# Four exponent buffers, an earlier first attention, and the second normalisation moved ahead of chunk 6's rounding

## What is computed

```
x = x + q8(layernorm(x)) @ q8(context)
x = x + mx_ffn(layernorm(x))            # silu(x Wg) * (x Wu), then Wd; weights fp4, rows fp6, blocks of 32
x = x + attention(layernorm(x), context)  # 32 query heads, 8 key/value heads of 128, rope, softmax
x = x + ffn(layernorm(x))               # 1376 hidden
```

## Time and profile before

| | |
|---|---|
| median of 3 runs | 683.6 us (683.54 to 683.84) |
| profiled execution | 683.66 us |
| its span | 681.9 us |
| PE busy | 659.7 us (97%) |
| DVE busy | 518.0 us (76%) |
| POOL busy | 471.5 us (69%) |
| ACT busy | 344.7 us (51%) |

### The profile page before, as it was taken

How to read it: one execution, slowest core, us unless ns; L and a number is a source line. 1 busy time by engine, 2 the same in 40 slices (tenths; PEclk the granted TensorE clock), 3 DMA queues, 4 the chain that set the end, 5 groups by cost and what they waited for, 6 DMA issues and landing times.

```text
span 681.9 us, 10810 instructions
## 1 busy us (share of the span) xinstructions
PE 659.7 (97%) x2993; PEld 484.8 (71%) x2996; DVE 518.0 (76%) x1024; ACT 344.7 (51%) x665; POOL 471.5 (69%) x435
## 2 busy tenths in 40 slices
PE   9998999899799999999999999999999999899998
PEld 3443444446567888888888888888888877788886
DVE  5999797997788888888888888888888886621113
ACT  1795223424656656656656656556656663221111
POOL 0688937337598688688788788698688477066661
PEclk9999999999999999999999999999999999999999
DMA  8999678403222222222222121222224012012321
GB/s 315 390 343 248 200 195 185 155 1 123 92 79 77 63 78 78 62 79 75 62 79 75 62 84 70 62 77 77 62 78 138 17 32 83 10 48 94 110 73 62
DMA packets 61260, 73.15 MB, mean 107 GB/s; under 512 B 25265, under 2 KB 33585, under 8 KB 60209
## 3 DMA queue, kind: packets, MB, share of 16 engines
q1 hardware_dynamic: 61232, 72.83, 34.7%
HBM read 58.00 MB, written 9.44 MB: 99 GB/s over the span
## 4 chain that ended last, share of the span: by engine, by line
PE 73%; DVE 12%; POOL 7%; issue 4%; ACT 2%; DMA 1%; SPq 0%; POOLq 0%; DVEq 0%; ACTq 0%
PE ps L687 16%; PE ps L689 16%; PE ps L688 16%; PE ps L755 11%; PE ps L721 7%; PE ps L572 3%; PE ps L540 2%; POOL mx_raw L1153 2%; PE ps L608 2%; POOL mx_w L1162 2%; DVE mx_amax L1416 1%; DVE stats L1329 1%; DVE xhat L1358 1%; POOL prob L1230 1%; DMA X<-in_x 1%
## 5 line engine op out<-in xcount | busy, mean ns | idle before, releaser
L1230 POOL TENSOR_SCALAR prob<-prob,rinv 128x512 f32<-128x512 f32 x128 | 89.4, 698 | 72.4 <-DVE rinv L1594 72.3
L1049 ACT ACTIVATE prob<-ps,nmax 128x512 f32<-128x512 f32 x128 | 88.3, 690 | 97.8 <-DVE nmax L1587 95.3
L755 PE MATMUL ps<-xt,wq_sb 128*128 128x512 f32 x384 | 103.1, 393 | 0.1
L1060 ACT CAST pT<-ps 128x512 fp32r<-128x512 f32 x128 | 75.1, 587 | 51.4 <-PE ps L721 50.4
L1587 DVE CUSTOM_DVE_ANT_0 ps<-ps,mask_sb 128x512 f32<-128x512 f32 x128 | 87.8, 686 | 5.1 <-PE ps L689 5.0
L1610 DVE TENSOR_TENSOR pT<-ps,pT 128x512 fp32r<-128x512 f32 x128 | 86.2, 674 | 3.0 <-ACT pT L1060 2.0
L755 PEld LDWEIGHTS ps<-xt,wq_sb 128*128 128x128 f32 x384 | 71.8, 188 | 17.2 <-issue 1.0
L721 PE MATMUL ps<-idf,prob 128*128 128x128 f32 x512 | 76.7, 272 | 0.4 <-POOL prob L1230 0.3
L721 PEld LDWEIGHTS ps<-idf,prob 128*128 128x128 f32 x512 | 63.8, 142 | 17.3 <-POOL prob L1230 1.6
L687 PE MATMUL ps<-pT,vt 128*128 128x512 f32 x128 | 61.2, 478 | 0.9 <-DVE pT L1610 0.9
L540 PE MATMUL ps<-ctxT,wk_sb 128*128 128x512 f32 x128 | 57.7, 594 | 0.0
(11 more groups left out here) (177 smaller groups left out, 1542.3 us busy)
## 6 DMA issues: line engine op xcount, KB each, us to landing
mx_raw<-in_mxw SPq DMA_DIRECT2D x8, 1024.0 KB, 6.9
wq_raw<-in_wq SPq DMA_DIRECT2D x32, 256.0 KB, 3.2
wo_raw<-in_wo SPq DMA_DIRECT2D x32, 256.0 KB, 2.6
v_scr<-v_st SPq DMA_DIRECT2D x16, 256.0 KB, 3.9
k_scr<-k_st SPq DMA_DIRECT2D x16, 256.0 KB, 3.4
kr<-k_scr SPq DMA_DIRECT2D x16, 256.0 KB, 2.8
kr_swp<-k_scr SPq DMA_DIRECT2D x32, 128.0 KB, 3.3
vr<-v_scr SPq DMA_DIRECT2D x16, 256.0 KB, 3.4
```

The lines of the kernel that those rows point to most:

```text
L755: last = mm(query_bank(H), wq_sb[:, par, l, k], xt[:, r, k], start=(n == 0), stop=(n == 11))
L1049: nc.scalar.activation(prob[:, j], bank(j % 2), ACT.Exp, bias=nmax[:, j:j + 1], scale=-1.0, accum_out=rsum[:, j:j + 1]).then_inc(exps, 1)
L1060: copy(pT[:, v % 2, 0, :, i * P:(i + 1) * P], bank(2 + i % 2).rearrange("p (k c) -> p k c", k=4)).then_inc(ph_ready, 1)
L1230: nc.gpsimd.tensor_scalar(prob[:, i], prob[:, i], rinv[:, i:i + 1], 1.0, ALU.mult, ALU.mult).then_inc(probs, 1)
```

## The change

- `mx_e` has four buffers, so that `mx_exponents(i)` waits for `scale_out` of chunk i-4.
- The clip of the first rows goes from DVE to POOL, behind `scale_in(1)`.
- DVE's `attention0` stands at the end of steps 3 and 4, where it was in steps 4 and 5. It adds the product to X first; POOL's `rows_add` adds the share behind it (`l0_read`), and moves from before `scale_out(3)` and `scale_out(4)` to before `scale_in(6)` and `scale_in(7)`. ACT's `share(0)` stands ahead of `context_keep(1)`.
- The second `layernorm`, with its fp6 part, stands ahead of the rounding of chunk 6.
- SP issues `chunk_turn(5)` ahead of the stores of k41, v60 and v61, and the rows' transposes ahead of v61, v70.
- Third stage: the mask operation of score 0 stands earlier on DVE, its exponential ahead of the swap copies of head 2 on ACT, POOL's sine product of head 0 between the two halves of head 2's weight split, and one of three late key products one unit earlier on PE.

```diff
--- before
+++ after
@@ -60,6 +60,7 @@
 NRAW = 3
+NEXP = 4
 ROTATE = (4, 5, 6, 7)
@@ -150,7 +151,7 @@
             mx_amax = sb("mx_amax", [P, CH // BLK], F32, a)
-            mx_e = sb("mx_e", [P, NRAW, CH // BLK], F32, a)
+            mx_e = sb("mx_e", [P, NEXP, CH // BLK], F32, a)
             mx_r = sb("mx_r", [P, NRAW, CH // BLK], F32, a)
@@ -413,12 +414,11 @@
             first_keys_load()
-            stores(STEPS[5][1] + STEPS[6][0])
             chunk_turn(5)
-            stores(STEPS[6][1])
+            stores(STEPS[5][1] + STEPS[6][0][:1])
             rows_turn_again(0)
             rows_turn_again(1)
-            stores(STEPS[7][0])
+            stores(STEPS[6][0][1:] + STEPS[6][1] + STEPS[7][0])
             k_load(6)
@@ -783,8 +783,8 @@
                     query(U, u, j)
-                    if isinstance(U, int) and U == -1 and j == 3:
-                        late_keys(4, range(1, 4))
+                    if isinstance(U, int) and U in (-2, -1) and j == 3:
+                        late_keys(4, range(1, 2) if U == -2 else range(2, 4))
                     if j % 2 == 0:
@@ -970,8 +970,8 @@
             copy_keys(2, 1)
+            share(0)
             context_keep(1)
-            share(0)
             copy_values(4, 0)
@@ -1061,6 +1061,8 @@
                 for j in range(4):
+                    if isinstance(U, int) and U == 0 and j == 0:
+                        exponent(0, 0, 0)
                     if j == 0 and within(U + 2, NH):
@@ -1078,7 +1080,8 @@
                     probs_high(U, u, j)
-                    exponent(U, u, j)
+                    if not (isinstance(U, int) and U == 0 and j == 0):
+                        exponent(U, u, j)
                     if j == 2 and within(U + 2, NH):
@@ -1146,7 +1149,7 @@
                 pool.wait_ge(mx_expo, i + 1)
-                ts(mx_r[:, p, 0:m].bitcast(I32), mx_e[:, p, 0:m].bitcast(I32), -1.0, -(2.0 ** 24), ALU.mult, ALU.add).then_inc(mx_scale, 1)
+                ts(mx_r[:, p, 0:m].bitcast(I32), mx_e[:, i % NEXP, 0:m].bitcast(I32), -1.0, -(2.0 ** 24), ALU.mult, ALU.add).then_inc(mx_scale, 1)
                 pool.wait_ge(mx_scale, i + 1)
@@ -1156,7 +1159,7 @@
                     pool.wait_ge(WT_in[i - 2], 16)
-                p, e = i % 2, i % NRAW
+                p, e = i % 2, i % NEXP
                 for cols in halves(i):
@@ -1181,16 +1184,20 @@
                     pool.wait_ge(l0_shared, t + 1)
+                    pool.wait_ge(l0_read, t + 1)
                     tt(X[:, t], X[:, t], xhat[:, t], ALU.add).then_inc(l0_added, 1)
...
             scale_in(1)
+            pool.wait_ge(q1_rounded, 1)
+            rows = xhat[:].rearrange("p t d -> p (t d)")
+            ts(rows, rows, ROUND, ROUND + 255.0, ALU.max, ALU.min).then_inc(q1_clipped, 1)
             for i in range(NFULL):
+                if i in (L0_AT, L0_AT + 1):
+                    rows_add(i - L0_AT)
                 if i + 2 <= NFULL:
                     scale_in(i + 2)
-                if i in (L0_AT - 1, L0_AT):
-                    rows_add(i - L0_AT + 1)
                 scale_out(i)
@@ -1200,9 +1207,11 @@
-            def split(high, low, raw, h_done, l_done, count):
+            def split(high, low, raw, h_done, l_done, count, between=None):
                 pool.sem_inc(pool_past_wait, 1)
                 nc.gpsimd.tensor_scalar(high, raw, 1.0, 1.0, ALU.mult, ALU.mult).then_inc(h_done, 1)
+                if between:
+                    between()
                 pool.wait_ge(h_done, count)
@@ -1213,12 +1222,17 @@
-            def query_split(U, u, g):
+            def query_sine(U):
+                pool.wait_ge(q_swapped, U + 3)
+                tt(q_swp[:].rearrange("p (b c) -> p b c", b=BATCH), q_swp[:].rearrange("p (b c) -> p b c", b=BATCH),
+                   ropeQ[:, 1].unsqueeze(1).to_broadcast([P, BATCH, SEQ]), ALU.mult).then_inc(q_sined, 1)
+
+            def query_split(U, u, g, between=None):
                 H, par = U + 4, u % 2
...
                     after(pool, q_sums, H - 1)
-                    split(wq_sb[:, par, 0], wq_sb[:, par, 1], wq_raw[:, par], wqh_ready, wq_split, H + 1)
+                    split(wq_sb[:, par, 0], wq_sb[:, par, 1], wq_raw[:, par], wqh_ready, wq_split, H + 1, between)
@@ -1228,12 +1242,12 @@
                         nc.gpsimd.tensor_scalar(prob[:, i], prob[:, i], rinv[:, i:i + 1], 1.0, ALU.mult, ALU.mult).then_inc(probs, 1)
-                    if isinstance(U, int) and U in (-2, -1) and j == 0:
-                        query_split(U, u, g)
-                    if j == 0 and within(U + 2, NH):
-                        pool.wait_ge(q_swapped, U + 3)
-                        tt(q_swp[:].rearrange("p (b c) -> p b c", b=BATCH), q_swp[:].rearrange("p (b c) -> p b c", b=BATCH),
-                           ropeQ[:, 1].unsqueeze(1).to_broadcast([P, BATCH, SEQ]), ALU.mult).then_inc(q_sined, 1)
+                    if isinstance(U, int) and U == -2 and j == 0:
+                        query_split(U, u, g, lambda: query_sine(-2))
+                    elif j == 0 and within(U + 2, NH):
+                        if isinstance(U, int) and U == -1:
+                            query_split(U, u, g)
+                        query_sine(U)
                     if j == 1 and not (isinstance(U, int) and U in (-2, -1)):
@@ -1382,10 +1396,6 @@
-            def clip_rows():
-                dve.wait_ge(q1_rounded, 1)
-                ts(rows(xhat[:]), rows(xhat[:]), ROUND, ROUND + 255.0, ALU.max, ALU.min).then_inc(q1_clipped, 1)
-
             def clip_context(b):
@@ -1402,7 +1412,6 @@
                     dve.wait_ge(l0_sums, 2 * b + t % 2 + b + 2)
-                    dve.wait_ge(l0_added, t + 1)
                     stt(X[:, t], bank(rotating(("l", b, t % 2 + 1))), sx[:, 4:5], X[:, t], ALU.mult, ALU.add).then_inc(l0_read, 1)
@@ -1416,8 +1425,8 @@
             def mx_exponents(i):
-                p, m = i % NRAW, width(i) // BLK
-                after(dve, mx_ready, 2 * (i - NRAW + 1))
+                p, m = i % NEXP, width(i) // BLK
+                after(dve, mx_ready, 2 * (i - NEXP + 1))
                 dve.wait_ge(mx_peak, i + 1)
@@ -1465,15 +1474,10 @@
             for i in range(NFULL):
-                if i != L0_AT + 2:
-                    mx_round(i, 0)
-                    mx_round(i, 1)
+                mx_round(i, 0)
+                mx_round(i, 1)
                 if i + 2 <= NFULL:
                     mx_peaks(i + 2)
-                if i in (L0_AT, L0_AT + 1):
-                    attention0(i - L0_AT)
-                if i == 0:
-                    clip_rows()
                 if i == 2:
@@ -1484,10 +1488,10 @@
                     mx_exponents(i + 2)
+                if i in (L0_AT - 1, L0_AT):
+                    attention0(i - L0_AT + 1)
                 if i == L0_AT + 1:
-                    mx_round(i + 1, 0)
-                    mx_round(i + 1, 1)
-                    dve.wait_ge(l0_read, NT)
+                    dve.wait_ge(l0_added, NT)
                     layernorm(False)
@@ -1568,6 +1572,14 @@
+            def row_max(U, u, j):
+                n = 4 * U + j
+                dve.wait_ge(scores, n + 1)
+                dve.sem_inc(dve_past_wait, 1)
+                nc.vector.tensor_tensor_reduce(out=bank(j % 2), in0=bank(j % 2), in1=mask_sb[:, 2 * (u % 2) + j % 2],
+                                               scale=-1.0, scalar=BIG, op0=ALU.add, op1=ALU.min,
+                                               accum_out=nmax[:, j:j + 1]).then_inc(rowmax, 1)
+
             def unit(U, u, g):
@@ -1579,14 +1591,8 @@
                         tt(oT[:, u % 2, 1], bank(4 + u % 2), oT[:, u % 2, 0].bitcast(F32), ALU.subtract).then_inc(o_split, 1)
-                    if within(U, NUNIT):
-
-                        n = 4 * U + j
-                        dve.wait_ge(scores, n + 1)
-                        dve.sem_inc(dve_past_wait, 1)
-                        nc.vector.tensor_tensor_reduce(out=bank(j % 2), in0=bank(j % 2), in1=mask_sb[:, 2 * (u % 2) + j % 2],
-                                                       scale=-1.0, scalar=BIG, op0=ALU.add, op1=ALU.min,
-                                                       accum_out=nmax[:, j:j + 1]).then_inc(rowmax, 1)
+                    if within(U, NUNIT) and not (isinstance(U, int) and U == 0 and j == 0):
+                        row_max(U, u, j)
@@ -1613,6 +1619,8 @@
                         tt(q_cos[:], q_cos[:], q_swp[:], ALU.add).then_inc(q_roped, 1)
+                    if isinstance(U, int) and U == -1 and j == 2:
+                        row_max(0, 0, 0)
                     if j == 2 and within(U + 2, NH):
```

## The result

The changed kernel takes **694.57 us** (median of 4 runs, 693.62 to 694.84) beside 683.72 for the kernel before on the same chip (4 runs, 683.54 to 684.21): ratio 1.0155, 95% interval 1.0137 to 1.0173. It is slower, as forecast, but by 10.9 us and not by 5; the forecast's range ended at 690.8. The profiled execution has a span of 692.6 and a mean granted clock of 0.992 (before 681.9 and 1.000).

The account below looks back on a forecast made before the run. PE-bound, busy 659.7 of 681.9 us, with gate_up's start as the gate: 683.66 + 5.1 (gate_up at 116.1, not 111.04) - 0.1 (third stage) = 688.7, median 0.06 lower, so 688.6 us; range 684.0 to 690.8.

Parts of the forecast that it names:

- (b): Clip of 1.22 us leaves DVE for a free place on POOL; chunk pipeline moves up by about 1.1 us.
- the clock behind the gap: PE after its 7.6 us gap before v71: slower clock loses 1.7 us, bounded by 0 and 3.4.
- the third stage: Mask, exponential, sine and late-product edits after gate_up: -0.1 us, ends -1.9 and +1.2.
- (a): First attention drains earlier: three PE waits of 4.3 us together go, v71 could start at 98.1, not 102.4.
- T: End of chunk 6's rounding on DVE: forecast 104.1, where it was 86.2.
- at least as much as it saved: Case for POOL's clip: without cover between scale_in(1) and scale_in(2), it costs POOL at least what it saved.
- The normalisation against POOL: DVE's second normalisation starts at 80.2, waits for POOL's instructions of 1.9 us, and ends at 99.3.
- rival 2: DVE loses one turn of 1.9 us less to POOL: T 102.2, gate_up 114.2, 686.7 us; chance 0.13.
- Who waits for T: ACT's lifts and k41's copy, PE's v71 (T + 1.6 = 105.7) and SP's key loads wait for chunk 6's rounding.
- T + 12.0: Start of gate_up on PE counted from the end of chunk 6's rounding: T 104.1 gives 116.1.
- SP: Six key loads wait for T; behind them the rows' transpose lands at T + 11.1 = 115.2.

Follow-up runs that it names:

- e1: The changed kernel with the clip of the first rows back on DVE; 691.30 us, ratio 1.0109 to the kernel before.
- e11: The changed kernel with POOL's max and min on xhat replaced by multiply by 1 and add 0; 689.77 us, ratio 1.0091 to the kernel before.
- e5: The changed kernel with clip and second normalisation both back in their old places; 686.68 us, ratio 1.0046 to the kernel before.
- e2: The changed kernel with chunk 6 rounded ahead of the second normalisation again; 689.12 us, ratio 1.0079 to the kernel before.
- e10: The changed kernel with unit v70's products repeated once and a half more, filling PE's wait before v71; 694.08 us, ratio 1.0150 to the kernel before.
- e4: The kernel before with all the third stage's edits and nothing else of the change; 684.89 us, ratio 1.0015.
- e13: e6 with chunk 8's peaks, chunk 6's clip and chunk 8's exponents right behind the second normalisation on DVE; 681.51 us, ratio 0.9963 to the kernel before.
- e8: The kernel before with only the second normalisation moved ahead of chunk 6's rounding; 691.42 us, ratio 1.0109.
- e3: The changed kernel with unit v70 computed twice, filling part of PE's wait before v71; 694.09 us, ratio 1.0146 to the kernel before.
- e6: The changed kernel with clip, second normalisation and third stage all put back; 685.96 us, ratio 1.0029 to the kernel before.

## Why the prediction was right, and where it failed

The direction was right, and so were the waits that were forecast; the time lies 3.8 us above the stated range. The step that failed is (b), POOL's clip taken as free; two terms were mis-sized besides, the clock behind the gap and the third stage.

- **(a) The attention's waits go: right.** v71 could start at 98.1, I wrote; without the clip on POOL (e1) the values before it end at 87.57 + 10.46 = 98.03. What I did not ask is what is late next if only this is done: DVE's rounding of chunk 7, at the same 109 us. In the change itself T hid it.
- **(b) The clip: this step failed.** "The chunk pipeline moves up by about 1.1 us" had POOL's clip hidden in a free place of unstated length. The place was 4.69 us long, by a row of the kernel before that my sum did not use; the clip took 7.07, and the normalisation began at 84.29, not 80.2. That the rest of the step held is shown by e11, which has no clip of xhat at all: there it began at 79.95, 0.9 before e1, where the clip is on DVE. I had named the case ("at least as much as it saved") and given it no price and no rival; the nearest rows, multiplications on POOL, were of other operations.
- **The normalisation against POOL: right, 1.1 us too dear.** Three small rows waited (1.32, 1.83, 1.83), and it took 18.0 us to the rounding's start where I had 19.1; undisturbed it takes 13.7 (85.73 to 99.44 in e5). Of the 1.1, 0.7 are a slip in my sum: four POOL instructions of 1.9 us from 80.6 end at 88.2, and I wrote 88.9. The row at 90.43 has two inputs of SBUF and took 1.83 us beside POOL, where the same operation took 0.16 at 92.69 with POOL at rest. So the rule of the Trainium skill ("SBUF — State Buffer", "SBUF: two separate sides") that I leaned on, by which such a row too waits for GpSimd's whole instruction, agrees with a row now, and rival 2, one turn fewer, is out.
- **Who waits for T: right.** k41's copy ended at T + 1.63 and v71 started at T + 1.68 (I had 1.6). The gap was 5.3 us and not 7.6, because T came 3.1 us later and PE 5.4 (103.5 for 98.1), mostly by its wait at 58.73 and the slow matmuls behind it: with the late pipeline the rows' transposes for the first attention are late (e2 puts the same wait down to q1T). That delay lay inside the later wait: in the change itself it cost nothing.
- **The clock: right in kind, mis-sized.** v71 lost 3.1 us, not 1.7; inside my bound of 3.4. With T + 12.0 forecast and T + 13.2 measured this is the other part of the miss at `gate_up`. How little of it reaches the end is what e10 shows: without the slow unit 694.08, 0.5 us less.
- **SP: right, 0.8 short.** T + 11.1 for the transposes; in e10, where PE was ready, T was 106.86 and `gate_up` came at 118.81, T + 11.95. Chunk 5's transpose took 3.2 us, not 2.8.
- **The third stage: wrong, +1.3 for -0.1.** I took the value between ends of two edits as if they added. I had the third mask operation within 0.1 us of its old place in the stage; it came 1.4 later (187.85 - 169.80 against 177.08 - 160.44). Each edit is zero alone; together the one takes away the slack that the other used. e4 shows 1.0 us of the 1.3; the other 0.3 stay open.
- **The sum.** Start of the normalisation +4.1, its length -1.1, the clock and the rest behind T +1.3, third stage +1.4: 688.6 + 5.7 = 694.3, against 694.57.

By removal the clip is worth 3.3 us, the normalisation 5.5, both together 7.9 (by the ratios 3.1, 5.2 and 7.5). The 0.9 between 8.8 and 7.9 is less than the spread of e2's runs, so whether the two overlap is not shown.

## What to carry to other kernels

A "free place" in an engine's list is a length in microseconds: before moving an instruction there, find a row of that engine with the same operation, and if there is none, make the missing price a rival. Where a wait is removed and the time stands still, look for a second gate that ended at the same moment; e13 needed both, and either alone gave nothing. One of the two was moved there by three edits together (the earlier attention, four buffers, SP's order), which no run takes apart. Before an urgent row is put behind a long one, list who waits for it on every other engine.

## What the runs showed of the hardware

- POOL's tensor_scalar with max and min on 128x2048 f32 took 7.07 us, with mult and add 1.90; DVE's max and min took 1.22. A DVE clip of bf16 that began meanwhile took 4.90 instead of 0.68 us and ended 0.55 us behind POOL's row; DVE's reduction of 128x2048 beside it took its usual 2.28.
- How much the clock takes does not follow the length of the wait. A unit of 3.47 us took 6.56 after 5.32 us of standing still, 5.85 after 7.39 (e1), 5.10 after 3.62 (e8), 5.40 after 2.14 (e3), and 3.70 after 0.30 (e10). A wait of 1.91 for an exponential was followed by full speed in the kernel before and by a clock of 0.64 in the profiled execution of e13. Runs of one kernel differ in this: e6's spread over 3.4 us and e2's over 2.9, and the longer times have the lower clock. "TensorE: Matmul & The Clock Gate" of the Trainium skill, Part 1, says that an idle TensorE falls back to 1.2 GHz; the 6.56 us, nearly twice 3.47, agree.
